# Attended values of a wide cross-attention as sixteen 64x64 products on quarters of the TensorE array, in place of four full-array products against a block-diagonal operand

## The reference, cut to what matters

```
qh = (q_in @ wq + bq).reshape(b, q_len, H, K)          # H = 16 heads, K = 128 dims
kh = (kv_in @ wk + bk).reshape(b, t, H, K)
vh = (kv_in @ wv + bv).reshape(b, t, H, K)
kh = concatenate([kh, bias_k]);  vh = concatenate([vh, bias_v])   # one more key and value
weights = softmax(einsum('bqhk,bthk->bhqt', qh, kh) / sqrt(K))
ctx = einsum('bhqt,bthk->bqhk', weights, vh).reshape(b, q_len, H * K)
return ctx @ wo + bo
```

## Time and profile before

| | us |
|---|---|
| median of 3 runs (lowest, highest) | 2432.32 (2425.67, 2437.57) |
| the profiled execution's own time | 2433.81 |
| its span, first to last instruction | 2432.0 |
| TensorE busy in it | 2240.4 (92%) |
| loads of stationary operands busy | 1774.0 (73%) |
| DVE / ACT / POOL busy | 1236.7 / 959.8 / 320.7 |

### The profile page before, as it was taken

How to read it: one execution, slowest core, us unless ns; L and a number is a source line. 1 busy time by engine, 2 the same in 40 slices (tenths; PEclk the granted TensorE clock), 3 DMA queues, 4 the chain that set the end, 5 groups by cost and what they waited for, 6 DMA issues and landing times. The chain is left out here.

```text
span 2432.0 us, 41151 instructions
## 1 busy us (share of the span) xinstructions
PE 2240.4 (92%) x15874; PEld 1774.0 (73%) x15874; DVE 1236.7 (51%) x2696; ACT 959.8 (39%) x2593; POOL 320.7 (13%) x626
## 2 busy tenths in 40 slices
PE   6899898999998999999999799999999979788975
PEld 5778787787776777777777577777777767666753
DVE  6857775765561333333333233333333326888686
ACT  2343345545343333333333233333333334444442
POOL 1011111000000000000000000000000013333340
PEclk9999999999999999999999899999999989898987
DMA  6000000020004200000000300000000010000000
GB/s 233 4 15 28 15 21 14 21 96 13 7 10 159 76 13 13 13 13 0 13 13 5 74 5 13 13 13 13 0 13 13 5 31 1 10 9 6 9 1 14
DMA packets 60088, 62.98 MB, mean 26 GB/s; under 512 B 16000, under 2 KB 57024, under 8 KB 58304
## 3 DMA queue, kind: packets, MB, share of 16 engines
q1 hardware_dynamic: 59968, 61.29, 7.8%
HBM read 50.79 MB, written 10.49 MB: 25 GB/s over the span
## 5 line engine op out<-in xcount | busy, mean ns | idle before, releaser
L1415 ACT ACTIVATE l2a_exps<-l2a_ps_s,l2a_shift 128x65 f32<-128x65 f32 x512 | 154.5, 315 | 299.8 <-DVE l2a_shift L1475 299.8
L1404 ACT ACTIVATE l2a_qT<-l2a_ps_q,cols 128x256 f32<-128x256 f32 x256 | 107.6, 471 | 392.9 <-PE l2a_ps_q L1549 392.9
L1601 PE MATMUL l2a_ps_y<-shared,l2a_oT 128*128 128x256 f32 x1024 | 242.4, 380 | 1.1 <-ACT l2a_oT L1421 1.1
L1463 DVE TENSOR_SCALAR l2a_kT<-l2a_ps_k,cols 128x256 f32<-128x256 f32 x256 | 112.1, 480 | 194.6 <-PE l2a_ps_k L1549 193.5
L1601 PEld LDWEIGHTS l2a_ps_y<-shared,l2a_oT 128*128 128x128 f32 x1024 | 184.6, 190 | 21.3 <-ACT l2a_oT L1421 1.5
L1489 DVE COPY l2a_pT<-l2a_ps_p 64x256 f32<-64x256 f32 x256 | 107.9, 421 | 122.4 <-PE l2a_ps_p L1580 120.7
L1471 DVE TENSOR_REDUCE l2a_row_max<-l2a_ps_s 128x4 f32<-128x260 f32 x128 | 54.9, 429 | 191.7 <-PE l2a_ps_s L1572 191.7
L1590 PE MATMUL l2a_ps_o<-l2a_pT,l2a_v 128*128 128x128 f32 x1024 | 148.1, 288 | 0.0
L1378 POOL TENSOR_TENSOR l2a_learned<-l2a_exps,l2a_inv_sum 128x4 f32<-128x4 f32 x128 | 26.1, 204 | 872.2 <-DVE l2a_probs L1482 872.2
L1590 PEld LDWEIGHTS l2a_ps_o<-l2a_pT,l2a_v 128*128 128x128 f32 x1024 | 124.0, 191 | 8.8
L1549 PEld LDWEIGHTS l2a_ps_k<-l2a_cT,l_wk 128*128 128x128 f32 x512 | 97.9, 191 | 38.3 <-issue 27.8
(11 more groups left out here) (265 smaller groups left out, 4413.8 us busy)
## 6 DMA issues: line engine op xcount, KB each, us to landing
f_c_tile<-in_ctx SPq DMA_DIRECT2D x16, 256.0 KB, 2.8
between<-f_final SPq DMA_DIRECT2D x16, 256.0 KB, 2.2
l2a_c_tile<-in_ctx SPq DMA_DIRECT2D x16, 256.0 KB, 2.7
shared<-in_l_wo SPq DMA_DIRECT2D x2, 2048.0 KB, 17.7
inside<-l2a_y_out SPq DMA_DIRECT2D x16, 256.0 KB, 2.2
f_x_tile<-in_x SPq DMA_DIRECT2D x8, 256.0 KB, 7.2
shared<-in_l_w SPq DMA_DIRECT2D x2, 1024.0 KB, 9.4
l_mlp_w<-in_l_mlp_w SPq DMA_DIRECT2D x2, 1024.0 KB, 10.2
```

Source lines behind the costliest of these rows:

```text
L1404: last = nc.scalar.activation(qT[:, n, :], ps_q[:, n * ROUND:(n + 1) * ROUND], ACT.Identity, bias=col(f"l2_bq{a + 1}", 2 * p + n), scale=1.0)
L1415: nc.scalar.activation(exps[:, m, :], ps_s[:, m * KEYS:(m + 1) * KEYS], ACT.Exp, bias=shift[:, m:m + 1], scale=scale, accum_out=row_sum[:, ...
L1463: last = nc.vector.tensor_scalar(kT[:, n, :, 0:SEQ], ps_k[:, n * ROUND:(n + 1) * ROUND].rearrange("d (m k) -> d m k", k=SEQ), col(f"l2_bk{ ...
L1601: nc.tensor.matmul(ps_y[:, u * DIM:(u + 1) * DIM], oT[:, n, u].rearrange("d b q -> d (b q)"), wo[:, 2 * p + n, :], start=(p == 0 and n == ...
```

## The change

`attend` now makes 16 products where it made 4. For each n and b, for each sequence half u and for each half of the 128 value dims, it multiplies 64 keys by 64 dims (the stationary operand) with 64 keys by 64 queries. The row half of the array is given by the keys' partitions (u), the column half by the partitions of the output (dims), so that four consecutive products stand on the four quarters of the array. The results of u=0 go to `ps_o[:, 0:256]`, those of u=1 to `ps_p[:, 256:512]`: two banks. `pT` loses its second index and its zeros. The transposes of the learned probabilities move from `ps_p` to `ps_x`. As `attend` writes into the bank of the transposes, `transpose_probs` waits as well until ACT has copied the previous pair's results (`o_ready`), and `attend` waits for the setting up (`set_up`).

```diff
-        pT = sb("pT", [P, 2 * NB, NU, SEQ])
+        pT = sb("pT", [P, 2 * NB, SEQ])
+        o_half = [ps_o[:, 0:ROUND], ps_p[:, ROUND:2 * ROUND]]
...
-            nc.gpsimd.memset(pT[:], 0.0).then_inc(set_up, 1)
...
             def attended_out(i, p):
                 act.wait_ge(o_in_psum, per_pair(i, p))
-                for n in range(2):
-                    last = nc.scalar.activation(oT[:, n], ps_o[:, n * ROUND:(n + 1) * ROUND].rearrange("d (b u q) -> d u b q", b=NB, u=NU),
+                for u in range(NU):
+                    last = nc.scalar.activation(oT[:, :, u].rearrange("d n b q -> d n (b q)"), o_half[u].rearrange("d (n t) -> d n t", n=2),
                                                 ACT.Copy)
...
-                    last = nc.vector.tensor_copy(pT[half, :, u, :], ps_p[half, 0:ROUND].rearrange("k (m q) -> k m q", q=SEQ))
+                    last = nc.vector.tensor_copy(pT[half], ps_p[half, 0:ROUND].rearrange("k (m q) -> k m q", q=SEQ))
...
             def transpose_probs(i, p):
                 pe.wait_ge(p_ready, per_pair(i, p))
+                if p:
+                    pe.wait_ge(o_ready, per_pair(i, p - 1))
+                elif not isinstance(i, int) or i:
+                    pe.wait_ge(o_ready, per_pair(i - 1, PAIR - 1))
...
             def attend(i, p):
                 g, first = divmod(2 * p, 4)
+                pe.wait_ge(set_up, 6)
                 pe.wait_ge(pT_ready, per_pair(i, p))
...
                 for n in range(2):
                     for b in range(NB):
-                        last = nc.tensor.matmul(ps_o[:, n * ROUND + b * P:n * ROUND + (b + 1) * P],
-                                                v[g % 2][b][:, (first + n) * WIDE:(first + n + 1) * WIDE],
-                                                pT[:, n * NB + b].rearrange("k u q -> k (u q)"), start=True, stop=True)
+                        at = n * NB + b
+                        for u in range(NU):
+                            keys_of = slice(u * SEQ, (u + 1) * SEQ)
+                            for dims in (slice(0, WIDE // 2), slice(WIDE // 2, WIDE)):
+                                d = (first + n) * WIDE + dims.start
+                                last = nc.tensor.matmul(o_half[u][dims, at * SEQ:(at + 1) * SEQ], v[g % 2][b][keys_of, d:d + WIDE // 2],
+                                                        pT[keys_of, at], start=True, stop=True)
...
-                    last = nc.tensor.transpose(ps_p[:, ROUND + u * P:ROUND + (u + 1) * P], learned[:, u, :], ident)
+                    last = nc.tensor.transpose(ps_x[:, u * P:(u + 1) * P], learned[:, u, :], ident)
```

More of the change, by code:

```diff
@@ L1361, in _ @@
             nc.gpsimd.memset(learned[:], 0.0).then_inc(set_up, 1)
-            nc.gpsimd.memset(pT[:], 0.0).then_inc(set_up, 1)
+            pool.wait_ge(set_up, 5)
+            nc.gpsimd.memset(learned[:, :, ONES:ONES + 1], 1.0).then_inc(set_up, 1)
             pool.wait_ge(set_up, 6)
-            nc.gpsimd.memset(learned[:, :, ONES:ONES + 1], 1.0).then_inc(set_up, 1)
-            pool.wait_ge(set_up, 7)
             norm.inverse_deviations(pool, 0)
@@ L1426, in learned_transposed @@
                 act.wait_ge(learnedT_in_psum, count(i, 1, 0))
-                nc.scalar.activation(learnedT[:].rearrange("h u q -> h (u q)"), ps_p[:, ROUND:2 * ROUND], ACT.Copy
+                nc.scalar.activation(learnedT[:].rearrange("h u q -> h (u q)"), ps_x[:, 0:ROUND], ACT.Copy
                                      ).then_inc(learnedT_ready, 1)
@@ L1517, in slot @@
                 if j == -1:
-                    dve.wait_ge(set_up, 7)
+                    dve.wait_ge(set_up, 6)
                     dve.wait_ge(folded_in_psum, 1)
```

## The result

| | before | after |
|---|---|---|
| median of the runs of both on one chip, us | 2429.57 (4 runs, 2425.67 to 2437.57) | 2398.68 (4 runs, 2397.15 to 2402.99) |
| profiled execution, us (its span) | 2433.81 (2432.0) | 2398.87 (2397.1) |

What follows compares the result with a forecast made beforehand. TensorE's list was taken as the bound: `attend` with its way out falls from 0.995 to 0.73 us a pair, 0.265 us 128 times is 33.9 us, so 2433.8 becomes 2399.9; forecast 2400 us, range 2394 to 2422.

Steps and rivals of the forecast that it cites:

- What bounds: In the wide attentions TensorE's list is the bound, with least slack 1.0 us; time taken out of `attend` comes off one for one.
- 128 times: The 0.265 us gain per pair counts in 2 calls, 8 rounds and 8 pairs, 33.9 us in all.
- The step of 0.058 to 0.059 and four quarters at once: In `attend`, passes on one quarter start 0.058 to 0.059 us apart and four quarters overlap: 0.48 us first to last, from 0.885.
- whatever is streamed up to 65 columns: In `attend`, the step on one part stays 0.058 to 0.059 us for any stream up to 65 columns.
- The way out, 0.15 + 0.10: Between `attend` and the values: 0.15 us to their first pass plus 0.10 for its load in the open; before, 0.11.
- The slot with the learned transposes: The slot holding two transposes of learned probabilities falls from 9.04 us, scores to scores, to 8.78.
- Pay the same way out: Learned transposes, moved to another bank with the same count, pay the same cost behind `attend` as the values do.
- Waits, copies, memset at zero: Added TensorE waits, ACT's and DVE's copies in new forms, and the dropped zeroing of pT change the time by zero.
- Rival A: Slower: the array cannot be fed four quarters at once in `attend`; +5 to +20 us, 2439 to 2454; chance 0.08.
- Rival B: The loop's longer list no longer fits; 12 jumps back wait 0.5 us each, 2406, at most 2434; chance 0.08.
- Rival C: No gain: another wait ends last, or TensorE's clock drops with less array at work; 2425 to 2440; chance 0.04.

## Why the prediction was right

- **What bounds**: TensorE's list, one for one. Right in 14 of the 16 rounds: 0.27 us a slot came off, with 1.00 of busy time and clock in both windows. "128 times" was too many. The last round of each call is bound at its end by DVE's probabilities, and there the gain was 0.3 us in all instead of 4.4; the prediction's windows did not reach into it. That the spans still differ by 34.9 us, against the 33.9 forecast, is luck: 3 us came from places that the change does not touch. The forecast of 2400 also started from a profiled execution 4 us above the median that was then measured for the kernel before; from medians the gain is 30.9 us.
- **The step of 0.058 to 0.059 and four quarters at once**: right, 0.48 us forecast and measured. This was the step on which all hung, carried over from the scores (step) and from L2377 and L1091 (overlap). The reason I gave for the step, "whatever is streamed up to 65 columns", was borne out with 32 columns.
- **The way out, 0.15 + 0.10**: right. 1015.01 to 1015.16, and 1.98 against 1.88. The experiment with `attend` behind the values shows the same two terms by themselves. Without these terms the halved steps (0.41 us a pair) would have given 2381.
- **The slot with the learned transposes**: forecast 8.78, measured 8.73. "Pay the same way out" was wrong by 0.05: two transposes stood between `attend` and the values before too, and their own first load in the open costs about 0.05 (997.02 to 997.29 is 0.27, where two such passes took 0.22 with the load hidden; a transpose here is one pass, not two), not 0.10. It comes once in 8 slots, 0.8 us in all.
- **Waits, copies, memset at zero**: right; the kernel with only the waits took 0.9986 (0.9972 to 1.0000). The copies and the memset were not tried by themselves; ACT and DVE are within 2 us of their busy time before.
- **Rival A** (0.08) is refuted by the sustained 0.0146 us a pass. **Rival B** (0.08) did not come, with 1317 instructions in the loop. But it was nearer than I had it: 256 instructions more bring it into one of two loops. Its price was too low as well. I took 0.5 us a jump, since 2.3 us of queued work lies in front, with a bound of 2.8; measured are 0.5 to 2.3 us in one wait, and 4.2 in two. **Rival C** came in small: in both windows no wait took the place (200.00 of 200 us, clock 1.00), but at the end of each call the wait for DVE grew from 1.65 to 2.11 us and the clock fell behind it. The kernel with `attend` behind the values has the same wait (4.2 us in two) without such a fall there, so the fall need not follow.

## What to carry to other kernels

Small products gain from parts of the array only if load and stream both shrink: a step takes the longer of the two (0.112 us for 128 columns loaded, 0.109 for 128 streamed, 0.058 for 64 loaded). Let consecutive products go round the parts, and count for each change of shape 0.10 us of draining and a load in the open, 0.05 us for 64 columns or 0.10 for 128; here the way out took back 0.14 of the 0.41 us that the steps gave. Do not multiply a gain by all slots before you have looked at the ones at the ends of a loop: another engine can be the bound there. Before a loop's body is made longer, look at the instruction packets and at waits for "issue" behind the jump back.

## What was not expected of the hardware

- The order of the same 16 products was worth 103 us (first to last 1.32 instead of 0.48 us).
- A row half of the array loads 128 columns no quicker than the whole: 0.112 us a pass in both.
- Twice the work on the quarters showed no limit of the feed (0.0146 us a pass, and so over 96 passes too), yet eighths stall after about 32 passes. The cause is open.
- TensorE's list in a loop stops being kept somewhere above 1317 instructions, at 1573 in one loop and not in the other; each jump then costs 0.5 to 4.2 us of idle time, and in some rounds a lower clock behind it.

Not tried: two pairs' `attend` in one go, which would halve the changes of shape, and quarters of the two row halves in one bank.
